# Moving q's maximum, the residual additions, the context snapshot and q's transposes within the step of a fused linear-attention and FP4-FFN kernel

## The reference

```python
xn = layernorm(x)
# attention: 16 heads of 16, causal over buckets of 64 tokens
q, k, v = split(xn @ W_qkv.T)          # per head
q = softmax(q) * 16 ** -0.5 ; k = exp(k)
context = exclusive_cumsum_over_buckets(k^T v) ; ksum = exclusive_cumsum_over_buckets(sum k)
attn = (q @ context) / max(q . ksum, 1e-6)
# FFN: both operands of every product are rounded to FP4 in blocks of 16 channels,
# scale = max|x| / 6, values to the grid 0, .5, 1, 1.5, 2, 3, 4, 6
h = silu(fp4(xn) @ fp4(w_gate).T) * (fp4(xn) @ fp4(w_up).T)     # 704 wide
out = x + attn @ W_out.T + fp4(h) @ fp4(w_down).T
```

## Time and profile before

| what | value |
|---|---|
| median of 3 runs | 1360.46 us |
| the profiled execution | 1361.72 us, its span 1360.0 us |
| DVE busy, instructions | 1309.7 us (96%), 3901 |
| PE busy | 1271.1 us (93%) |
| ACT busy | 969.4 us (71%) |
| POOL busy | 355.0 us (26%) |
| chain that ended last | DVE 52%, issue 33%, DVEq 7%, PE 5%, ACT 2% |
| granted TensorE clock, mean | 0.989 of full |

### The profile page before, as it was taken

How to read it: one execution, slowest core, us unless ns; L and a number is a source line. 1 busy time by engine, 2 the same in 40 slices (tenths; PEclk the granted TensorE clock), 3 DMA queues, 4 the chain that set the end, 5 groups by cost and what they waited for, 6 DMA issues and landing times.

```text
span 1360.0 us, 41012 instructions
## 1 busy us (share of the span) xinstructions
PE 1271.1 (93%) x9934; PEld 871.0 (64%) x9934; DVE 1309.7 (96%) x3901; ACT 969.4 (71%) x3221; POOL 355.0 (26%) x791
## 2 busy tenths in 40 slices
PE   0279999999999999999999999999999999999996
PEld 0157666666666666666666666666666666666664
DVE  6869999999999999999999999999999999999996
ACT  1567777777777777777777777777777777777772
POOL 2212223222222323222222222223232222323220
PEclk9889999999999999999999999999999999999998
DMA  4024544444454444444544444545454454445444
GB/s 129 12 40 82 108 98 100 105 100 102 98 114 100 101 105 98 103 100 98 113 101 105 98 102 99 112 98 104 105 109 99 92 115 101 96 105 110 97 83 91
DMA packets 432380, 133.64 MB, mean 98 GB/s; under 512 B 397404, under 2 KB 431836, under 8 KB 432348
## 3 DMA queue, kind: packets, MB, share of 16 engines
q1 hardware_dynamic: 431622, 132.60, 46.8%
q10 hardware_dynamic: 726, 0.72, 0.2%
HBM read 19.99 MB, written 16.78 MB: 27 GB/s over the span
## 4 chain that ended last, share of the span: by engine, by line
DVE 52%; issue 33%; DVEq 7%; PE 5%; ACT 2%; DMA 1%; SPq 0%; ACTq 0%
DVE hx_v L880 7%; DVE ga L810 5%; DVE blk L834 3%; DVE xring L963 3%; DVE hx_v L887 3%; DVE h L820 2%; DVE drec L794 2%; DVE xq_s L935 2%; DVE q_rows L922 2%; DVE att L799 2%; DVE osum L958 2%; DVE blk L843 1%; DVE dz L786 1%; DVE hrow L854 1%; DVE dmx L790 1%
## 5 line engine op out<-in xcount | busy, mean ns | idle before, releaser
L418 POOL TENSOR_TENSOR xn_s<-xn,xn_s 128x256 f16<-128x256 f32 x128 | 108.6, 848 | 820.3 <-ACT xn_s L535 820.3
L1165 PE MATMUL outp<-w_down_cat,q_rows 128*128 128x256 f16 x1408 | 246.1, 274 | 0.0
L617 ACT ACTIVATE snap<-ctxp,mask 64x68 f32<-64x68 f32 x1024 | 236.5, 310 | 3.3
L1165 PEld LDWEIGHTS outp<-w_down_cat,q_rows 128*128 128x128 f16 x1408 | 138.3, 98 | 16.5
L1167 PE MATMUL outp<-w_down_lo,q_rows 128*128 128x256 f16 x640 | 147.6, 274 | 0.0
L580 ACT ACTIVATE th<-unit0a,c_g 128x352 f32<-128x352 f32 x128 | 71.0, 554 | 97.3 <-PE unit0b L1078 95.3
L556 ACT ACTIVATE qexp<-qsh,c_q 128x256 f32<-128x256 f32 x128 | 65.1, 508 | 99.0 <-DVE qsh L773 98.8
L580 ACT ACTIVATE th<-unit1a,c_g 128x352 f32<-128x352 f32 x128 | 71.0, 555 | 87.4 <-PE unit1b L1078 65.0
L827 DVE TENSOR_REDUCE blk<-h 128x44 f32<-128x704 f32 x128 | 123.8, 967 | 0.1
L411 POOL TENSOR_TENSOR att_s<-att,att_s 128x256 f16<-128x256 f32 x128 | 87.9, 687 | 108.1 <-ACT att_s L572 108.1
L880 DVE TENSOR_TENSOR hx_v<-h,blk 128x704 f32<-128x704 f32 x128 | 111.0, 868 | 0.0
(11 more groups left out here) (199 smaller groups left out, 4059.0 us busy)
## 6 DMA issues: line engine op xcount, KB each, us to landing
xring<-x SPq DMA_DIRECT2D x128, 128.0 KB, 2.7
out<-xring SPq DMA_DIRECT2D x128, 128.0 KB, 2.5
xnt<-xn_s SPq DMA_TRANSPOSE x128, 2.5
xqt<-xq_s SPq DMA_TRANSPOSE x128, 2.4
att_t<-att_s SPq DMA_TRANSPOSE x128, 2.5
q_rows<-q_rows SPq DMA_TRANSPOSE x128, 3.6
raw_qkv<-wqkv_t SPq DMA_DIRECT2D x1, 768.0 KB, 4.4
raw_up<-wup ACTq DMA_DIRECT2D x2, 352.0 KB
```

What stands on the lines that cost most here:

```text
L418: nc.gpsimd.tensor_tensor(xn_s[:, par, 1, :], xn[:, par, :], xn_s[:, par, 0, :], ALU.subtract).then_inc(xn_lo, 1)
L617: nc.scalar.activation(kept[:, :, cols], sums[:, :, cols], ACT.Copy, scale=mask[rows, f, h:h + 1])\
L1165: nc.tensor.matmul(downp, hqt[:, par, m, :], w_down_cat[:, m, :], start=(m == 0), stop=False)
```

## The change

Nothing is computed in another way, and no instruction that computes is added or removed; calls are moved in three of the lists. Semaphores and their values stay the same.

```diff
# ScalarE step
                 tanh_gate(k, 0, par)
+                snapshot(k + 1)
                 normalise_waits(k + 3)
                 mean_waits(n, d + 4)
                 tanh_gate(k, 1, par)
                 factor_of_row(k - 1, odd)
                 normalise(n, d + 3)
                 mean_of(n, d + 4)
+                squares_wait(k + 4)
                 high_xn(k + 3, odd)
-                squares_wait(k + 4)
+                squares_of(n, d + 4)
                 copy_qt(k + 1, odd)
-                squares_of(n, d + 4)
-                snapshot(k + 1)
# VectorE step
                 block_max_h(k - 1, odd)
+                max_q(k + 1, odd)
                 block_scales(k - 1, k + 2)
-                max_q(k + 1, odd)
+                add_up(n, d - 3, 0)
                 over_one(k - 1, k + 2)
                 row_scale(k - 1)
                 shift_q(k + 1, odd)
                 over_row(k - 1)
+                add_up(n, d - 3, 1)
                 over_scales_h(k - 1, odd)
                 over_scales_x(k + 2, par)
                 round_hx(k - 1, k + 2, 0)
-                add_up(n, d - 3, 0)
                 round_hx(k - 1, k + 2, 1)
-                add_up(n, d - 3, 1)
# TensorE step
                 gate_up(k, 1, par)
-                transpose_q(k + 1, odd)
                 project_att(k - 2, par)
                 project_h(k - 2, par)
+                transpose_q(k + 1, odd)
```

## The result

The changed kernel takes 1364.66 us (median of 8 runs) against 1361.15 us for the kernel before (8 runs, of which three are those shown above). The ratio is 1.0024, with a 95% interval of 1.0014 to 1.0035: slower by a quarter of a per cent. The forecast was 1361.6 with a range of 1346 to 1379.

What follows compares the result with a forecast made beforehand. VectorE bounded the kernel before; the round by GpSimd was to set the changed step: (9.93 - 9.904) x 118 = +3.1, less 2, is +1.1 on 1361.72, so 1362.8, in medians 1361.6 us; 8-in-10 range 1346 to 1379.

Steps and rivals of the forecast that it cites:

- The mechanism named as the likeliest: Steady step: the round by GpSimd sets it at 9.93 us, L843 stalled some 0.1 in every step; chance 0.47.
- the prediction's own sign: Stated test on VectorE: L843 at its 0.153 in most steps would show the prediction wrong and the first rival right.
- the first rival: L411 ends before L843 asks; VectorE alone sets the step at 9.78 to 9.86, 1343.9 to 1353.3 us; chance 0.28.
- VectorE's order up to q's shift: VectorE, early in the step: q's maximum goes ahead of L843, which starts at 1.95, and L773 at 3.16.
- ScalarE's chain from q's shift: ScalarE after L773: first tanh +1.35, snapshot +1.80, second tanh +3.69, mean +4.82, xn_s +5.34; moved wait costs 0.13.
- GpSimd's chain: GpSimd, counted from q's shift: L418 at +5.82, then the small operations, L411 at +8.15 with no idle ahead.
- The cost of the two passes back to back: VectorE, L901 to L909 without osum between: +0.12 to 0.20 a step, making VectorE's own step 9.78 to 9.86.
- the round through ScalarE and GpSimd: From one L773 to the next by ScalarE and GpSimd: 9.88 us, with 0.05 for register waits and loop branch 9.93.
- L418 into the next step's start: GpSimd's L418 would hold VectorE's L933; step 9.99 to 10.1, 1369 to 1382 us; margin 0.08; chance 0.22.
- TensorE's own step: TensorE: at most 9.65 us a step, transposes costing the same at the end; chance 0.03 that it becomes the bound.
- TensorE's wait for L963 goes and pays nothing: TensorE: 29.5 us of waiting for VectorE's L963 goes, without gain, as VectorE is later than TensorE.
- Start and end: Outside the steady steps: earlier last L963 and first snapshots take 2 us off, from 0 to 4.

Runs made afterwards that it cites:

- the kernel with the wait last: Changed kernel with the wait for the first rounding pass's result (hx_step) put last of three ahead of L909: 1344.57 us, ratio 0.9882.
- the cut L411: L411 computing 64 of 256 columns: in the kernel before 1335.95 us, ratio 0.9823; in the changed kernel 1363.97 us, ratio 1.0025.
- The last experiments: Changed kernel, second addition between the passes, GpSimd's small operations behind the next L411: 1337.52 us; also q's transposes back: 1331.27; also ScalarE's second half as before, except snapshot: 1330.92.

## Why the prediction was right, and where it was not

The time came out, 1364.66 for 1361.6 and inside the range; the sign had been left open (0.39 faster, 0.40 slower). The mechanism named as the likeliest did not come out: by the prediction's own sign, L843 at its 0.153 in most steps, it is the first rival that happened, at a time outside that rival's range.

- *VectorE's order up to q's shift*: right. L843 starts at 1.96 to 1.99 of the step (1.95 foreseen) and L773 at 3.13 to 3.16 (3.16 foreseen).
- *ScalarE's chain from q's shift*: right to 0.1. First tanh +1.35 (328.27 - 326.92), snapshot +1.80, second tanh +3.69, mean +4.82, all as worked out; xn_s +5.43 for 5.34. The wait for the accumulator cost 0.22 and not 0.13. The register waits behind the snapshot cost nothing: the second tanh follows it by 0.03.

```profile
328.27 0.55 ACT L580 ACTIVATE th<-unit1a,c_g 128x352 f32<-128x352 f32 x1
328.72 1.86 ACT L617 ACTIVATE snap<-ctxp,mask 64x68 f32<-64x68 f32 x8
330.61 0.55 ACT L580 ACTIVATE th<-unit0a,c_g 128x352 f32<-128x352 f32 x1
...
332.35 0.42 ACT L535 ACTIVATE xn_s<-xn 128x256 f16<-128x256 f32 x1
```

- *GpSimd's chain*: the start right (L418 +5.92 for 5.82), the spacing too wide. Where GpSimd is never idle, L426 follows L418 by 0.63, not 0.75, and L411 follows L436 by 0.14, not 0.27, in one kind of step. L411 comes 8.05 behind q's shift in the mean (7.93 and 8.16 in the two kinds of step) for 8.15.
- *The cost of the two passes back to back*: this is the term that was mis-sized. Put at 0.12 to 0.20, taken from an early step outside the loop, it is 0.30. In that early step L909 starts 0.04 behind the end of L901, as in the kernel with the wait last, so the row held the dependence alone. The prediction named the two register instructions and allowed 0.08 for them; the wait-last experiment shows that they cost 0.18. VectorE's own step is 9.94, not 9.78 to 9.86.
- *What sets the step*: wrong. It was to be the round through ScalarE and GpSimd at 9.93, with L843 held by 0.1. It is VectorE's own list, at 9.946, and the cut L411 changes nothing. The round is shorter than was counted: with 8.05 for 8.15, L843's end 0.70 behind it and 1.03 to the next shift, and nothing lost at the register waits, it is 9.78, and 9.775 is the step where it does rule (the second addition put back). That the time came out is luck: the round was put 0.15 too long, VectorE's list some 0.1 too short, and the larger of the two came out nearly the same. The first rival, "the lock is missed", was right about the lock, with a price that was wrong by the same term.
- *L418 into the next step's start*: rightly put as less likely. L418 ends at 333.51, 0.25 before the next L933. The margin of 0.08 was taken from a step of 9.73, which no row gives and which is shorter than the 9.78 to 9.86 worked out for VectorE.
- *TensorE's own step*: put at 9.65 at most, with the transposes at the same cost in either place. The last experiments show 9.67, and 9.72 with the transposes at the end. It did not matter below 9.946.
- *TensorE's wait for L963 goes and pays nothing*: right; the row has no counterpart in the waits after.
- *Start and end*: -2.1 for -2.

## What to carry to other kernels

When an operation is moved away from between two that depend on each other, look at what stands between wait and instruction in the order: let the wait that is satisfied last be the last, on the instruction itself. And where a GpSimd operation can hold VectorE, the phase between the two is a cost like any other: find for each long GpSimd operation which VectorE operation it meets. In these traces the reductions L834 and L827 kept their 0.41 and 0.97 under L411, and the operations that read PSUM (L764, L799, L810, L820) kept theirs under L411 or L418, in every kernel. So move the GpSimd operation over those, before trying orders on VectorE. Parts of a change that shift such a phase can't be judged one by one.

## What the runs showed of the hardware

- In the loops of this kernel several waits in front of one operation stand on several instructions (L906, L908 and L909 in the chain of waits above), and only those ahead of the wait that is satisfied last are hidden: 0.18 us where two instructions stand behind it, at L909, and 0.09 where one does, at L901.
- The dependence of L909 on L901 costs 0.12 by itself: 0.70 from start to start with the wait last, 0.58 with an addition between them.
- The loser of the port waits for nearly the whole of the other's operation (L843, asking 0.05 behind the start of a 0.68 us L411, took 0.66), and a GpSimd operation that waits can get in between two VectorE operations that follow each other: L418 at 509.98 waited for the first L922 and held the second. The 0.67 us operation then cost each side 0.3 to 0.4.
- Time in which a VectorE operation is held counts into its duration and into VectorE's busy time. The shortest and the median length of one line, side by side, show it (0.153 and 0.232 for L843 before).
- One-column GpSimd operations held VectorE nowhere in these traces by more than 0.03, though VectorE held them by 0.08 to 0.28 (L429 took 0.27 at 323.85, where it takes 0.19 alone, beside L933 at 323.79 + 0.28; L426 took 0.47 in the kernel with VectorE's moves alone).
- The two transposes on TensorE cost 0.22 us from start to start ahead of the attention projection and 0.27 at the end of the step.
